# A decoder of six blocks on one core: the scan's channel blocks in pairs, attention heads over three banks of PSUM

## The reference

```
xn  = layernorm(x); xh, z = split(xn @ W_in)           # 512 channels each
xc  = silu(causal_conv(xh, 4 taps)); B, C, d = xc @ W_xp; dt = softplus(d @ W_dt + b_dt)
h_t = exp(dt*A) * h_(t-1) + dt*B*xc                    # 512 channels x 16 states
out = ((sum_n h*C + xc*D) * silu(z)) @ W_out + x       # 1: the scan
2: cosine similarity of a projection of x with one of ctx
3: feed-forward, 4 experts with LoRA, the top 2 by softmax weight (router)
4: attention, 16 heads of 64 on 4 key heads, rotary, LoRA on all projections
5: cross attention to ctx, one head, with its own layernorms
6: a gated recurrence over the batch axis, then tanh(x@wo + c@uo + bo)
```

## Time and profile before

| | |
|---|---|
| median of 3 runs | 1385.49 us (1383.58 to 1388.08) |
| the profiled execution | 1379.84 us, its span 1377.9 us |
| mean granted clock of TensorE | 0.936 |
| busy | PE 1160.8, DVE 1056.9, ACT 794.5, POOL 290.7 us |
| DMA | 100.27 MB moved |

### The profile page before, as it was taken

The page is one execution under the profiler, slowest core; times in us unless marked ns, Lnnn a source line. Parts: engine busy times, 40 slices in busy tenths (PEclk is TensorE's granted clock), DMA queues, the critical chain, the costliest instruction groups (busy, mean ns, idle before and its releaser), DMA issues.

```text
span 1377.9 us, 16592 instructions
## 1 busy us (share of the span) xinstructions
PE 1160.8 (84%) x5760; PEld 921.4 (67%) x5760; DVE 1056.9 (77%) x1719; ACT 794.5 (58%) x1989; POOL 290.7 (21%) x341
## 2 busy tenths in 40 slices
PE   4697677888899799989998899988998989989852
PEld 2454456666678577866786678867786768868741
DVE  3998899899869797899879897998699763343216
ACT  3433545467658665677567756776477545536521
POOL 0000201222421333232313231324122420010001
PEclk9877999989999899999999999999999999999976
DMA  4612010234424424234414442533343320000301
GB/s 183 242 46 71 7 63 8 77 77 92 101 54 92 89 47 115 58 81 99 110 31 100 86 96 55 110 76 60 92 104 77 50 51 20 1 0 8 121 0 61
DMA packets 55285, 100.27 MB, mean 73 GB/s; under 512 B 5417, under 2 KB 28810, under 8 KB 54562
## 3 DMA queue, kind: packets, MB, share of 16 engines
q0 software_dynamic: 27648, 37.76, 16.8%
q1 hardware_dynamic: 27554, 61.46, 13.8%
HBM read 55.42 MB, written 6.04 MB: 45 GB/s over the span
## 4 chain that ended last, share of the span: by engine, by line
PE 40%; DVE 31%; DMA 9%; ACT 9%; issue 7%; POOL 4%; DVEq 0%; SPq 0%; ACTq 0%; POOLq 0%
PE bank L288 15%; DVE scans L520 10%; DMA scans<-scans 9%; PE bank L1105 4%; DVE scans L516 4%; DVE scans L523 4%; PE bank L1150 3%; PE bank L1123 3%; PE bank L475 2%; DVE nmax L1259 2%; DVE conv L399 2%; PE bank L671 2%; PE bank L883 2%; ACT scans L498 2%; PE bank L889 1%
## 5 line engine op out<-in xcount | busy, mean ns | idle before, releaser
L520 DVE TENSOR_TENSOR_SCAN scans<-scans 128x1024 f32<-128x1024 f32 x128 | 292.3, 2284 | 16.4 <-ACT scans L498 11.9
L498 ACT ACTIVATE scans<-dt,a_neg 128x255 f32<-128x255 f32 x512 | 221.4, 500 | 0.0
L475 PE MATMUL bank<-scans,ident 128*128 128x256 f32 x448 | 138.7, 432 | 49.9 <-DMA scans<-scans 27.0
L1193 ACT ACTIVATE ya<-bank,nmax 128x256 f32<-128x256 f32 x256 | 107.1, 472 | 86.1 <-DVE nmax L1259 86.0
L523 DVE TENSOR_TENSOR scans<-scans,BC 128x1024 f32<-128x1024 f32 x128 | 155.7, 1217 | 1.2
L1259 DVE TENSOR_REDUCE nmax<-bank 128x2 f32<-128x512 f32 x128 | 87.3, 683 | 90.2 <-PE bank L1105 89.1
L516 DVE TENSOR_TENSOR scans<-conv,BC 128x1024 f32<-128x1024 f32 x128 | 155.7, 1216 | 0.1
L552 POOL DMA_DIRECT2D scans<-scans x96 | 84.1, 876 | 289.1 <-DMA scans<-scans 287.8
L475 PEld LDWEIGHTS bank<-scans,ident 128*128 128x128 f32 x448 | 87.8, 210 | 85.5 <-DMA scans<-scans 38.9
L1123 PE MATMUL bank<-v,ya 128*128 128x65 f32 x1024 | 135.5, 278 | 4.4 <-ACT yo L1184 4.4
L1123 PEld LDWEIGHTS bank<-v,ya 128*128 128x128 f32 x1024 | 132.6, 201 | 8.3 <-issue 5.9
(11 more groups left out here) (255 smaller groups left out, 2229.6 us busy)
## 6 DMA issues: line engine op xcount, KB each, us to landing
BC<-xpj_scratch SPq DMA_DIRECT2D x32, 1024.0 KB, 6.1
scans<-scans POOLq DMA_DIRECT2D x96, 256.0 KB, 3.4
scans<-scans POOLq DMA_DIRECT2D x96, 128.0 KB, 2.7
xin<-in_x SPq DMA_DIRECT2D x8, 256.0 KB, 4.3
conv<-in_x SPq DMA_DIRECT2D x8, 256.0 KB, 2.9
out<-scans SPq DMA_DIRECT2D x8, 256.0 KB, 2.7
kept_x<-x SPq DMA_DIRECT2D x7, 256.0 KB, 2.0
kept_w<-wa SPq DMA_DIRECT2D x7, 256.0 KB, 2.0
```

Source lines behind the costliest of these rows:

```text
L475: last = pe.matmul(sums_of(c), ident[:, :], step_of(b, u)[:, i, :], start=False, stop=(h == UH - 1 and i == SUMMED[b] - 1), skip_group_che ...
L498: ins = act.activation(step[:, j, 1:S], dt[b % 2][:, c, 1:S], ACT.Exp, scale=a_neg[:, c, n:n + 1])
L520: dve.tensor_tensor_scan(flat(H[:, :, :]), flat(H[:, :, :]), flat(dBx), 0.0, ALU.mult, ALU.add).then_inc(s["a_scan"], 1)
L1193: act.activation(pe_[:, h % 2, t, :], YB[h % 2][:, t * S:(t + 1) * S], ACT.Exp, bias=nmax[:, h % 4, t:t + 1]).then_inc(s["t_p"], 1)
```

## The change

1. `UNITS`: pairs of channel blocks (0,1), then (2,3), in the outer loop; under each the four h. A round is two units with the same h. `BC` is loaded for each round: 8 times per batch and not 4, each time 1 MB, when the round before last is done.
2. Both pairs are summed in bank 1. The first pair is multiplied with silu(z) after unit 8; the skip matmuls of the second pair wait for that. ScalarE's tanh of the next batch's `xc` waits for the second skips. Tanh and product of `xc` take two channel blocks in one instruction.
3. Attention: `heads_in`, three banks (5, 6 and the freed bank 2). `turned` and `values` are one head later, scores of h wait for the copy of h-3, and in ScalarE's round the copy of i-2 comes ahead of the exponentials of i.
4. Norms: `stats` ends with bn_aggr; POOL makes var+eps and -mean by two tensor_scalar before pow. Each norm has its own small tiles.
5. Router: all pairs of scores are compared at once (128x32), the count of scores ahead is the rank.
6. `ORDER` is written out anew for all engines (PE 1108 letters for 1100, DVE 877 for 885, SP 123 for 91).

```diff
-UNITS = [(h, c) for h in range(UH) for c in range(EC)]
+UNITS = [(h, 2 * q + i) for q in range(EC // 2) for h in range(UH) for i in range(2)]
+ROUNDS = EC // 2 * UH
...
-            own.wait()
-            own.did(dve.tensor_scalar(ln_nm[tag][:, :], ln_mv[tag][:, :, 0], -1.0, None, ALU.mult))
-            return dve.tensor_scalar(ln_var[tag][:, :], ln_mv[tag][:, :, 1], EPS, None, ALU.add)
-
-        def rstd(pool, own, tag):
-            own.link(pool.tensor_tensor(ln_rs[tag][:, :], ln_var[tag][:, :], neghalf[:, 0:T], ALU.pow))
-            return pool.tensor_tensor(ln_nb[tag][:, :], ln_nm[tag][:, :], ln_rs[tag][:, :], ALU.mult)
+            return last
+
+        def rstd(pool, own, tag):
+            own.did(pool.tensor_scalar(ln_rs[tag][:, :], ln_mv[tag][:, :, 1], EPS, None, ALU.add))
+            own.did(pool.tensor_scalar(ln_nb[tag][:, :], ln_mv[tag][:, :, 0], -1.0, None, ALU.mult))
+            own.wait()
+            own.link(pool.tensor_tensor(ln_rs[tag][:, :], ln_rs[tag][:, :], neghalf[:, 0:T], ALU.pow))
+            return pool.tensor_tensor(ln_nb[tag][:, :], ln_nb[tag][:, :], ln_rs[tag][:, :], ALU.mult)
...
         def scan_sp(sp, b):
             sp.wait_ge(*of("a_store", b))
-            for h in range(UH):
-                if h >= 2:
-                    sp.wait_ge(*of("a_hC", b, EC * (h - 1)))
+            for r in range(ROUNDS):
+                if r >= 2:
+                    sp.wait_ge(*of("a_hC", b, 2 * (r - 1)))
                 elif b:
-                    sp.wait_ge(*of("a_hC", b - 1, EC * (h + 3)))
+                    sp.wait_ge(*of("a_hC", b - 1, 2 * (r + ROUNDS - 1)))
...
             for u, (h, c) in enumerate(UNITS):
+                if h == 0 and c % 2 == 0:
+                    if c:
+                        pe.wait_ge(*of("a_gated", b, 1))
+                    for i in range(2):
+                        last = pe.matmul(sums_of(c + i), skips[:, c + i, :], xc[:, c + i, :], start=(i == 0), stop=False, skip_group_check=True)
+                    last.then_inc(s["a_skip_ps"], 1)
+                    yield
...
-                if u == NU - 2:
-                    dve.wait_ge(*of("a_y_ps", b, NU - 2))
-                    dve.wait_ge(*of("a_silu_z", b))
+                if u == NU // 2:
+                    dve.wait_ge(*of("a_y_ps", b, NU // 2))
+                    dve.wait_ge(*of("a_silu_z", b, 1))
...
-            own.did(dve.tensor_reduce(sc2[:, 1, :], sm[:, 1, :, :], AX, ALU.add))
-            for i, (score, hit, rank, one) in enumerate([(1, 3, 4, 5), (6, 7, 8, 9)]):
-                top, best = 3 + 2 * i, 4 + 2 * i
-                own.link(dve.tensor_reduce(sc2[:, top, :], sm[:, score, :, :], AX, ALU.max))
...
+            own.did(dve.tensor_reduce(sc2[:, 1, :], score, AX, ALU.add))
+            own.link(dve.tensor_tensor(ahead, score.unsqueeze(2).to_broadcast(pairs), score.unsqueeze(3).to_broadcast(pairs), ALU.subtract))
+            own.link(dve.tensor_tensor(ahead, ahead, tie.rearrange("p (e j) -> p e j", e=NE).unsqueeze(1).to_broadcast(pairs), ALU.is_gt))
+            own.link(dve.tensor_reduce(rank, ahead, AX, ALU.add))
...
+        heads_in = [y0, y1, bank[2]]
...
-                if h >= 2:
-                    pe.wait_ge(*of("t_pT", b, h - 1))
+                if h >= 3:
+                    pe.wait_ge(*of("t_pT", b, h - 2))
...
-                if 1 <= i <= NQ:
-                    turned(i - 1)
+                if 2 <= i <= NQ + 1:
+                    turned(i - 2)
                     yield
-                if i >= 2:
-                    values(i - 2)
+                if i >= 3:
+                    values(i - 3)
```

More of the change, by code:

```diff
@@ L89 @@
+        "SSSWSWWWWWWWW"
     ),
@@ L310, in front_sp @@
             yield
-        SA = bank[1:3]
+        s0 = bank[1]
         def conv_bank(b, j):
-            return SA[1] if b == 0 and j == 1 else f0
+            return bank[2] if b == 0 and j == 1 else f0
         def front_pe(pe, b):
@@ L390, in front_dve @@
             dve.wait_ge(*of("a_x", b))
-            stats(dve, own, xin, "f", "a").then_inc(s["a_var"], 1)
+            stats(dve, own, xin, "a").then_inc(s["a_var"], 1)
             yield
@@ L464, in scan_pe @@
                 pe.wait_ge(s["prep_skips"], EC)
-            for c in range(EC):
-                last = pe.matmul(sums_of(c), skips[:, c, :], xc[:, c, :], start=(c % 2 == 0), stop=False, skip_group_check=True)
-            last.then_inc(s["a_skip_ps"], 1)
-            yield
             for u, (h, c) in enumerate(UNITS):
+                if h == 0 and c % 2 == 0:
[4 more added lines that the diff above has]
+                    last.then_inc(s["a_skip_ps"], 1)
+                    yield
                 if SUMMED[b] == HN:
@@ L753, in x_dve @@
             dve.wait_ge(*of("b_x2", b))
-            stats(dve, own, xb, "w", "b1").then_inc(s["x_var"], 1)
+            stats(dve, own, xb, "b1").then_inc(s["x_var"], 1)
             yield
@@ L785, in x_dve @@
[L785 to L790 removed]
+            pairs = [P, T, NE, NE]
@@ new lines, in x_dve @@
+            ahead = sm[:, 2:6, :, :].rearrange("p a t e -> p (a t e)").rearrange("p (t e j) -> p t e j", t=T, e=NE)
+            score, rank, first, second = [sm[:, i, :, :] for i in (1, 6, 8, 9)]
+            own.did(dve.tensor_reduce(sc2[:, 1, :], score, AX, ALU.add))
+            own.link(dve.tensor_tensor(ahead, score.unsqueeze(2).to_broadcast(pairs), score.unsqueeze(3).to_broadcast(pairs), ALU.subtract))
+            own.link(dve.tensor_tensor(ahead, ahead, tie.rearrange("p (e j) -> p e j", e=NE).unsqueeze(1).to_broadcast(pairs), ALU.is_gt))
@@ new lines, in x_dve @@
+            own.link(dve.tensor_reduce(rank, ahead, AX, ALU.add))
+            yield
+            own.did(dve.tensor_scalar(second, rank, 1.0, None, ALU.is_equal))
+            own.did(dve.tensor_scalar(first, rank, 0.0, None, ALU.is_equal))
+            own.did(dve.reciprocal(sc2[:, 2, :], sc2[:, 1, :]))
+            own.wait()
+            own.did(dve.tensor_tensor(sm[:, 7, :, :], second, score, ALU.mult))
+            own.did(dve.tensor_tensor(sm[:, 10, :, :], first, second, ALU.subtract))
+            own.wait()
@@ L791, in x_dve @@
+            own.did(dve.tensor_reduce(sc2[:, 5, :], sm[:, 7, :, :], AX, ALU.add))
+            for i, one in enumerate([9, 10]):
+                own.did(dve.tensor_tensor(low[:, i, :, :].rearrange("p t (e r) -> p t e r", e=NE),
+                                          low[:, 1, :, :].rearrange("p t (e r) -> p t e r", e=NE),
+                                          sm[:, one, :, :].unsqueeze(3).to_broadcast([P, T, NE, RK]), ALU.mult))
             own.wait()
@@ L1003, in z_dve @@
             dve.wait_ge(*of("c_res", b))
-            stats(dve, own, x5, "w", "c1").then_inc(s["z_var"], 1)
+            stats(dve, own, x5, "c1").then_inc(s["z_var"], 1)
             yield
@@ L1124, in values @@
                 last.then_inc(s["t_o_ps"], 1)
-            for i in range(NQ + 2):
+            for i in range(NQ + 3):
                 if i < NQ:
```

193 lines of the change are left out of this document (92 added, 101 removed).

## The result

The median went from 1386.78 us (1383.58 to 1391.38, 4 runs) to 1407.78 (1406.42 to 1415.12, 4 runs): ratio 1.016, 95% interval 1.0113 to 1.0206. That is slower, with the whole interval above 1, where 1375.5 and "faster" were forecast, and it lies outside the range of 1352 to 1399. All ratios here leave out executions in a slower state, which the medians of the runs contain, so a ratio isn't always the quotient of the two medians beside it. The profiled execution has a span of 1404.6 us (before 1377.9) and a mean granted clock of 0.922 (before 0.936).

What follows compares the result with a forecast made beforehand. TensorE (90% busy) and VectorE (87%) were taken to bound the middle, VectorE alone 42 to 200 us. Terms -15 (banks) -9 (VectorE) +4 (POOL) +10 (folds) gave -10: 1375.5 us, range 1352 to 1399.

Steps and rivals of the forecast that it cites:

- POOL's share: Norms: two added POOL instructions at 0.3 us each delay each norm by 0.4 us, felt ten times: 4 us more.
- the forecast's third rival: Gains cancelled by POOL's small norm instructions (+18 for +4) or a wait replacing the bank's: 1385 us, chance 0.15.
- BC's loads and the folds: Scan: doubled loads of B and C delay folds issued with them; 24 times 0.4 us for TensorE, 10 us more.
- the mark of 40: Scan: the prediction counted as wrong if the scan's wait for ScalarE passed 40 us.
- Banks and VectorE: Attention's third bank removes two thirds of a 33.2 us wait, net -15; 28 us less VectorE work (norms, router) gives -9.
- The router: Router: fewer dependent VectorE steps take it from 3.65 to 2.4 us, 10 us of VectorE over eight batches.
- The gate and one bank for the sums: Scan sums: first gate moved from unit 14 to 8, second skips waiting for it: costs nothing, 8 us at most.
- The folds decide: Rival: folds issued with loads make scans late (+15) and TensorE wait more (+9): 1399.5 us, chance 0.24.
- They cancel: Rival: POOL's small norm instructions at nearly 1 us (+18 for +4), or a replacement wait, cancel gains: 1385 us, chance 0.15.

Runs made afterwards that it cites:

- c_half_bc: Kernel after with norms as before, batch 0's evacuations spread as before, and every second load of B and C cut to 4 KB: 1372.1 us, ratio 0.993.
- a_half_bc: Kernel after with odd rounds' loads of B and C (except one) cut to 4 KB, nothing else undone: 1404.1 us, ratio 1.0152.
- a_start3: Kernel after with batch 0's LoRA evacuations spread over units 3 to 12 and batch 1's front taps moved to units 5 and 7: 1397.8 us, ratio 1.015.
- b_pool_after: Kernel before with two small POOL instructions and a wait added behind each norm's product, 64 times: 1405.7 us, ratio 1.0193.
- b_start_late: Kernel before with nine of batch 0's sixteen LoRA evacuations and their matmuls put between units 3 and 4: 1401.0 us, ratio 1.0146.
- b_norms_dve: Kernel before with POOL taken out of the norms, VectorE doing the product and a comparison in place of the power: 1378.8 us, ratio 1.0002.

## Why the prediction was wrong, step by step

The step that failed is *POOL's share*, "+4". I costed the two instructions by their duration (0.3 us, right for the median) as latency of the norm at ten places, and 18 us was my upper end. Measured alone it is +29 us on the kernel before, and 11 to 20 in the kernel after (1.016 to 1.0078; 1.015 to 1.0002). Two things were missed in it. The mean of 0.98 us for a product in the earlier trace rows was the sign that POOL's instructions are held, and I took the lower row as "nearer to most". Even the upper end of 18, by which the forecast's third rival had the gains cancelled, falls short of the 29. And I asked who waits for the norm, not who stands behind it: the folds, in POOL's queue, and behind a fold TensorE's whole queue.

A second term was missing altogether: the order of batch 0. I read the new order for the gates and the loads, not for what stands between two scans while VectorE is the bound, which the earlier trace rows had shown for 42 to 200 us. It is worth +20 on the kernel before and about 10 or more in the kernel after.

*BC's loads and the folds*, "+10": right in size, by c_half_bc (0.0072 of 1380 is 9.9 us); in the kernel after with its other losses a_half_bc couldn't show it. Where it shows I had wrong: PE's wait for the folds fell to 13.2 us, and the scan's wait for its exponentials rose from 11.9 to 31.0, near the mark of 40 that I had set; but 26.0 of it is still there in c_half_bc, so that wait isn't the folds' alone. The median time to landing of a 256 KB fold rose from 3.4 to 4.1 us.

*Banks and VectorE*, "-15 - 9": c_half_bc has the banks, the router and the order of pairs, and not the doubled loads, the norms or the gap: 0.993, about -10 us. The banks' wait did fall to 4.6 us, more than the two thirds assumed; the value of it with the router is 10 and not 18 or so. VectorE's 28 us by themselves gave -2.3 and -3.2 us, each within its interval of nothing, where 9 was taken. How the 10 divides stays open: the bank's loop alone wasn't run, since the written order is bound to it.

*The router* was estimated at 2.4 us and takes 1.7: 646.67 to 647.38 and 648.53 to 649.49 in the timeline of DVE, with other work between.

*The gate and one bank for the sums*, "nothing": no run speaks against it, none isolates it.

The four parts together: -10 (banks, router, pairs), +10 (loads), +10 or more (start), +11 to 20 (norms) against the 22 measured. Whether they simply add stays open. a_start3 has only one of two losses undone and gains 1 us, where the same start gains 10 once the norms are undone; that looks as if the later queue hid what the other loses, but the intervals allow the same gain in both. The rest of the new `ORDER`, behind batch 0, was run in no version by itself and stands in the -10 with everything else. *The folds decide* gave the right side and nearly the right time (1399.5), for a reason that was the smaller part: that is luck. *They cancel* had the right mechanism, POOL's small instructions at nearly 1 us, but its time was added up wrongly: -10 with 18 in place of 4 is +4, so 1389.5 and not 1385.

## What to carry to other kernels

An instruction added to an engine that issues DMAs is priced by what stands behind it in that queue, not by its length; look first for means far above medians on POOL beside a busy VectorE. Read a new written order where one engine is the bound, and look for any stretch in which its long work is interrupted by work that waits. Before calling a suspected cost free, see whether the intervals could show it at all, and take it away from a kernel in which the larger losses are undone; in the kernel after the loads looked free, with intervals as wide as the effect, and they cost some 10 us.

## What the hardware showed that I had not expected

- POOL's elementwise instructions of 128x2 end with the VectorE instruction beside them where that one reads two SBUF tensors: 0.22 us became 1.07 beside a product and 2.18 beside a scan.
- Lost time came together with a lower granted clock of TensorE, and the same matmuls then took longer: 1160.8 us at 0.936 and 1178.6 at 0.922. "TensorE's busy time isn't touched by the change" was wrong for that reason. It goes that way in other pairs too (b_pool_after 1176.7 us at 0.923), and the kernel after had 0.922 to 0.930 in its four runs. Which comes first isn't shown. Between 42 and 200 us TensorE did 105.7 us of work at 0.74 and not 113.4 at 0.83 (means between its two levels, 1.2 and 2.4 GHz), and b_start_late, with nothing but the gap, has 0.75 there; but b_norms_dve has 0.76 in the same stretch with no time lost, and runs of the kernel before alone spread from 0.924 to 0.948, the slower ones at the lower clocks.
